# Layer 2's routing one group earlier, 16 scatters in every second group, and the tile list and padding beside the last scatters

## What is computed

```python
# layer 2, attention: 16 heads of 8 features, 64 queries and 64 keys for each batch entry, a mask
score = einsum('bhqd,bhkd->bhqk', qh, kh) / sqrt(8); attn = softmax(where(mask == 0, -1e9, score))
x = x + tanh(g_xattn[2]) * (merge(attn @ vh) @ w_o.T + b_o)
# layer 2, feed-forward: a LayerNorm of a LayerNorm, router, the 2 best of 8 experts, 128 -> 512 -> 128
xn = layer_norm(x_in) * gamma + beta          # x_in is itself the normed x; it is also the residual
probs = softmax(xn @ router_w.T / 1.5); w, idx = top_k(probs, 2)
out = sum over the 2 chosen e of w_e * (silu(xn @ W1[e]) @ W2[e]); x = x + tanh(g_ffn[2]) * (out + x_in)
```

## Time and profile before

| | us |
|---|---|
| median of 3 runs | 3185.36 |
| lowest, highest | 3180.08, 3189.39 |
| profiled execution, device time | 3190.76 |
| its span, first to last instruction | 3189.0 |
| layer 2 attention's group 3 to 14, at TensorE | 1682 to 1978 |
| last scatter issued | 2073.8 |
| first matmul of layer 2's feed-forward tiles | 2095.4 |

### The profile page before, as it was taken

One profiled execution on the slowest core, in us unless ns is written; L12 is line 12 of the kernel. 1 busy time (PEld: TensorE's weight loads), 2 busy tenths in 40 slices (PEclk: granted clock), 3 DMA queues, 4 the chain that ended last, 5 costly groups with the idle time before them and its releaser, 6 DMA issues. The chain is left out here.

```text
span 3189.0 us, 63316 instructions
## 1 busy us (share of the span) xinstructions
PE 2487.6 (78%) x20966; PEld 1889.2 (59%) x20966; DVE 2069.1 (65%) x6419; ACT 1395.7 (44%) x2573; POOL 1154.8 (36%) x1149
## 2 busy tenths in 40 slices
PE   3588778858779999999778888169996688887766
PEld 0254444447767787877656666147774365666755
DVE  6477648868667766677559788333333577784578
ACT  1466610013256666656456555022221465563432
POOL 2355512321054555455401344700000556634711
PEclk9988889969889999999989888579998788898988
DMA  4200001132100000000020010111111111100001
GB/s 142 98 31 27 20 27 40 39 113 70 34 1 1 1 1 1 0 1 1 16 71 12 28 36 23 46 47 54 53 54 53 43 33 32 39 10 10 1 25 33
DMA packets 126020, 108.78 MB, mean 34 GB/s; under 512 B 15548, under 2 KB 105942, under 8 KB 124888
## 3 DMA queue, kind: packets, MB, share of 16 engines
q1 hardware_dynamic: 106840, 80.58, 8.3%
q0 software_dynamic: 8192, 16.79, 1.8%
q10 hardware_dynamic: 10752, 8.39, 0.8%
HBM read 70.59 MB, written 35.13 MB: 33 GB/s over the span
## 5 line engine op out<-in xcount | busy, mean ns | idle before, releaser
L1318 POOL TENSOR_TENSOR l1ffn_hid<-l1ffn_act 128x512 f32<-128x512 f32 x256 | 330.5, 1294 | 341.7 <-ACT l1ffn_act L1459 308.0
L1600 DVE SCALAR_TENSOR_TENSOR l1ffn_acc<-bank,l1ffn_w,l1ffn_acc 128x128 f32<-128x128 f32 x960 | 269.3, 343 | 150.0 <-PE bank L1403 142.7
L1403 PEld LDWEIGHTS bank<-l_w_ahead,l1ffn_hid 128*128 128x128 f32 x2048 | 265.2, 191 | 68.7 <-issue 49.9
L1403 PE MATMUL bank<-l_w_ahead,l1ffn_hid 128*128 128x128 f32 x2048 | 271.7, 276 | 37.9 <-DVE l1ffn_acc L1600 37.5
L1456 ACT ACTIVATE l1ffn_act<-scores,l1ffn_b 128x512 f32<-128x512 f32 x256 | 176.3, 689 | 203.6 <-PE scores L214 203.4
L2231 ACT ACTIVATE l_probs_t<-bank 128x512 f32<-128x512 f32 x256 | 140.4, 596 | 105.9 <-PE bank L229 104.8
L2299 DVE TENSOR_REDUCE l_top<-scores 128x16 f32<-128x1024 f32 x128 | 155.2, 1213 | 43.1 <-PE scores L2130 42.6
L212 PE MATMUL scores<-l1ffn_z_high,l1ffn_w_high 128*128 128x512 f32 x384 | 173.5, 452 | 0.0
L2302 DVE TENSOR_TENSOR l_probs<-scores,l_top 128x1024 f32<-128x1024 f32 x128 | 156.8, 1225 | 13.7 <-DVE l_top L2299 0.5
L229 PEld LDWEIGHTS bank<-ident,l_probs 128*128 128x128 f32 x1024 | 130.0, 155 | 49.2 <-issue 25.5
L923 DVE SCALAR_TENSOR_TENSOR l0moe_acc<-scores,l0moe_w_now,l0moe_acc 128x128 f32<-128x128 f32 x512 | 137.7, 344 | 32.6 <-PE scores L871 32.6
(11 more groups left out here) (440 smaller groups left out, 6284.5 us busy)
## 6 DMA issues: line engine op xcount, KB each, us to landing
l2ffn_xs<-scratch_l_in SPq DMA_DIRECT2D x136, 64.0 KB, 1.8
scratch_l_out<-l2ffn_y SPq DMA_DIRECT2D x34, 256.0 KB, 2.3
x_all<-scratch_x SPq DMA_DIRECT2D x32, 256.0 KB, 3.4
l_ctx_t<-in_ctx_t SPq DMA_DIRECT2D x32, 256.0 KB
l_w_ahead<-in_l_w SPq DMA_DIRECT2D x3, 2048.0 KB, 12.7
x_all<-in_x SPq DMA_DIRECT2D x16, 256.0 KB, 3.0
l0mix_ctx<-in_ctx SPq DMA_DIRECT2D x16, 256.0 KB, 3.3
scratch_x<-l0mix_x_out ACTq DMA_DIRECT2D x16, 256.0 KB, 2.3
```

The source lines that it names most:

```text
L1318: pool.tensor_tensor(hid[:, e % K], act1[:, e % K], act3[:, e % K], ALU.mult)\
L1403: mm = pe.matmul(bank[5 + k][:, t * D:(t + 1) * D], hid[:, e % K, t * P:(t + 1) * P], w2[:, e, :], start=True, stop=True)
L1600: mm = v.scalar_tensor_tensor(out=acc[:, t, :], in0=y, scalar=w[:, h, t, e:e + 1], in1=before, op0=ALU.mult, op1=ALU.add)
```

## The change

It does four things.

1. The routing's steps move. The transposes of the routed z go from s = 3 to s = 1 of group i = g + 3; the logits from s = 1 of g + 4 to s = 2 of g + 3; `choose_first` from s = 2 of an odd group to s = 3 of the even group before it; `choose_second` from s = 3 of the odd group to s = 1 of it; the rank product from s = 2 of an even group to s = 3 of the odd group before it; `place_chosen` from s = 3 of an even group to its s = 0. Each `before` wait keeps its place in the slot; the waits on the routing's own readers move with the products.
2. A chunk's 16 scatters are issued in four successive slots, four in each, from s = 1 of an even group (6 for the first chunk) to s = 0 of the next; `LAG` is 6.
3. The count, the tile list and the padding writes are made at the end of the attention phase: TensorE's and VectorE's after their last slot, SyncE's after the context loads. The two tables for them are loaded with the routing's constants.
4. `l2_ffn` loses these steps; its SyncE waits for the padding and the scatters and loads at once.

```diff
 class PickTwo:
...
-    LAG = 7
+    LAG = 6
...
         sp.wait_ge(self.filled, 5)
         for e in range(picks.E):
             r = picks.E * picks.stride + e * P
-            sp.dma_start(picks.rows_in[r:r + P, :], self.zeros[:, :]).then_inc(self.padded, DMA)
-        sp.wait_ge(self.padded, picks.E * DMA)
+            sp.dma_start(picks.rows_in[r:r + P, :], self.zeros[:, :]).then_inc(picks.padded, DMA)
+
+    def pad(self, sp):
+        picks = self.picks
+        sp.wait_ge(self.listed, 1)
+        for e in range(picks.E):
+            r = sp.value_load(self.pad_row[0:1, e:e + 1], min_val=0, max_val=picks.E * picks.stride - P)
+            sp.dma_start(picks.rows_in[bass.ds(r, P), :], self.zeros[:, :]).then_inc(picks.padded, DMA)
+        sp.wait_ge(picks.padded, 2 * picks.E * DMA)
+
+    def tensor_count(self, pe):
+        pe.wait_ge(self.route, (self.CHUNKS - 1) * self.STEPS + 14)
+        pe.wait_ge(self.rank_out, self.CHUNKS)
+        pe.matmul(self.chip.bank[7][:, 0:L2_E], self.picks.ones[:, :], self.picks.cum[:, :, self.T], start=True, stop=True)\
+            .then_inc(self.counted, 1)
+
+    def vector_list(self, v):
+        picks, E, NT = self.picks, L2_E, self.picks.NT
+        full, past, before, tile_e, numbers = self.full, self.past, self.before, self.tile_e, self.numbers
+        n_tiles, ends = picks.n_tiles, picks.ends
+        total = self.chip.bank[7][:, 0:E]
+        made = 0
+
+        def next_step(instruction):
+            nonlocal made
+            made += 1
+            instruction.then_inc(self.table, 1)
+            v.wait_ge(self.table, made)
+        v.wait_ge(self.counted, 1)
+        v.tensor_tensor(self.pad_row[:, :], total, picks.base[:, :], ALU.add).then_inc(self.listed, 1)
+        next_step(v.tensor_tensor(full[:, :, :], self.steps[:, :].unsqueeze(1).to_broadcast([P, E, TILES]),
+                                  total.unsqueeze(2).to_broadcast([P, E, TILES]), ALU.is_lt))
+        next_step(v.tensor_reduce(n_tiles[:, :], full[:, :, :], AX.X, ALU.add))
+        next_step(v.tensor_tensor_scan(ends[:, :], picks.ones[:, 0:E], n_tiles[:, :], 0.0, ALU.mult, ALU.add))
+        next_step(v.tensor_tensor(past[:, :, :], numbers[:, :].unsqueeze(2).to_broadcast([P, NT, E]),
+                                  ends[:, :].unsqueeze(1).to_broadcast([P, NT, E]), ALU.is_ge))
+        next_step(v.tensor_reduce(tile_e[:, :], past[:, :, :], AX.X, ALU.add))
+        v.tensor_scalar(picks.tile_of_e[:, :], tile_e[:, :], float(E - 1), None, ALU.min).then_inc(self.listed, 1)
+        next_step(v.tensor_tensor(past[:, :, :], past[:, :, :],
+                                  n_tiles[:, :].unsqueeze(1).to_broadcast([P, NT, E]), ALU.mult))
+        next_step(v.tensor_reduce(before[:, :], past[:, :, :], AX.X, ALU.add))
+        next_step(v.tensor_tensor(before[:, :], numbers[:, :], before[:, :], ALU.subtract))
+        next_step(v.tensor_scalar(before[:, :], before[:, :], float(P), None, ALU.mult))
+        v.scalar_tensor_tensor(out=picks.tile_row[:, :], in0=tile_e[:, :], scalar=float(picks.stride),
+                               in1=before[:, :], op0=ALU.mult, op1=ALU.add).then_inc(self.listed, 1)
+        v.wait_ge(self.listed, 3)
 
...
-        c, part = divmod(i - 7, 2)
-        if 0 <= c < self.CHUNKS:
-            if part == 0 and s == 0:
+        c, part = divmod((i - 6) * G + s - 1, 2 * G)
+        if part < G and 0 <= c < self.CHUNKS:
+            if part == 0:
                 pool.wait_ge(self.routed, c + 1)
-            n = c * self.T + part * G + s
-            for k in range(picks.K):
-                pool.indirect_dma_start(out=picks.rows_in,
-                                        out_offset=bass.IndirectOffsetOnAxis(ap=picks.slot_in[:, k, n:n + 1], axis=0),
-                                        in_=picks.z[:, n, :], in_offset=None).then_inc(picks.scattered, DMA)
+            for n in (c * self.T + part * 2, c * self.T + part * 2 + 1):
+                for k in range(picks.K):
+                    pool.indirect_dma_start(
+                        out=picks.rows_in,
+                        out_offset=bass.IndirectOffsetOnAxis(ap=picks.slot_in[:, k, n:n + 1], axis=0),
+                        in_=picks.z[:, n, :], in_offset=None).then_inc(picks.scattered, DMA)
 
     def turned_out(self, pe, i):
         if 0 <= i - 3 < GROUPS:
             pe.wait_ge(self.z_t_done, i - 2)
 
     def logits_out(self, pe, i):
-        if 0 <= i - 4 < GROUPS:
-            pe.wait_ge(self.logits_done, i - 3)
+        if 0 <= i - 3 < GROUPS:
+            pe.wait_ge(self.logits_done, i - 2)
 
     def ranks_out(self, pe, i):
-        c, odd = divmod(i - 6, 2)
+        c, odd = divmod(i - 5, 2)
         if odd == 0 and 0 <= c < self.CHUNKS:
             pe.wait_ge(self.rank_out, c + 1)
 
     def tensor(self, pe, i, s, before):
 
         picks, bank, T, E = self.picks, self.chip.bank, self.T, L2_E
-        if s == 3 and 0 <= i - 3 < GROUPS:
+        if s == 1 and 0 <= i - 3 < GROUPS:
             g = i - 3
             pe.wait_ge(self.z_done, g * G + G)
             before()
             transposes(pe, bank[7], [picks.z[:, g * G + t, :] for t in range(G)], self.chip.ident)\
                 .then_inc(self.z_turned, 1)
-        if s == 1 and 0 <= i - 4 < GROUPS:
-            g = i - 4
+        if s == 2 and 0 <= i - 3 < GROUPS:
+            g = i - 3
             pe.wait_ge(self.z_t_done, g + 1)
             before()
             for t in range(G):
...
                     mm = pe.matmul(bank[7][r, t * E:(t + 1) * E], self.z_t[:, t * P + b * S:t * P + (b + 1) * S],
                                    picks.wr[:, :], start=True, stop=True)
             mm.then_inc(self.gated, 1)
-        c, odd = divmod(i - 6, 2)
-        if s == 2 and odd == 0 and 0 <= c < self.CHUNKS:
+        c, odd = divmod(i - 5, 2)
+        if s == 3 and odd == 0 and 0 <= c < self.CHUNKS:
             pe.wait_ge(self.route, c * self.STEPS + 14)
             before()
             out = bank[7][:, 0:T * E].rearrange("p (t e) -> p t e", t=T)
...
 
     def scalar(self, act, i, s):
         bank, T, E = self.chip.bank, self.T, L2_E
-        if s == 3 and 0 <= i - 3 < GROUPS:
+        if s == 1 and 0 <= i - 3 < GROUPS:
             g = i - 3
             act.wait_ge(self.z_turned, g + 1)
             reuse(act, self.gated, g)
             act.activation(self.z_t[:, :], bank[7][:, :], ACT.Identity, bias=self.picks.beta[:, 0:1],
                            scale=self.picks.gamma[:, 0:1]).then_inc(self.z_t_done, 1)
-        if s == 1 and 0 <= i - 4 < GROUPS:
-            g = i - 4
+        if s == 2 and 0 <= i - 3 < GROUPS:
+            g = i - 3
             act.wait_ge(self.gated, g + 1)
             reuse(act, self.route, (g // 2 - 2) * self.STEPS + 2)
             act.activation(self.logits[:, g // 2 % 2, g % 2 * G:(g % 2 + 1) * G, :].rearrange("p t e -> p (t e)"),
                            bank[7][:, 0:G * E], ACT.Identity).then_inc(self.logits_done, 1)
-        c, odd = divmod(i - 6, 2)
+        c, odd = divmod(i - 5, 2)
         if odd == 0 and 0 <= c < self.CHUNKS:
             if s == 0:
                 act.wait_ge(self.route, c * self.STEPS + 2)
                 act.activation(self.prob[:, :, :], self.shifted[:, :, :], ACT.Exp, scale=1.0 / L2_TEMP)\
                     .then_inc(self.exped, 1)
-            if s == 2:
+            if s == 3:
                 act.wait_ge(self.ranked, c + 1)
                 reuse(act, self.route, (c - 1) * self.STEPS + 17)
                 act.activation(self.rank[:, :, :].rearrange("p t e -> p (t e)"), bank[7][:, 0:T * E], ACT.Identity)\
                     .then_inc(self.rank_out, 1)
 
     def vector_setup(self, v):
-        v.wait_ge(self.w_in, 7 * DMA)
+        v.wait_ge(self.w_in, 9 * DMA)
         v.wait_ge(self.filled, 5)
 
     def vector(self, v, i, s):
...
             self.vector_stats(v, i - 2)
         if s == 0 and 0 <= i - 3 < GROUPS:
             self.vector_apply(v, i - 3)
+        c, odd = divmod(i - 4, 2)
+        if s == 3 and odd == 0 and 0 <= c < self.CHUNKS:
+            self.choose_first(v, c)
         c, odd = divmod(i - 5, 2)
-        if odd == 0 and 0 <= c < self.CHUNKS:
-            if s == 2:
-                self.choose_first(v, c)
-            if s == 3:
-                self.choose_second(v, c)
+        if s == 1 and odd == 0 and 0 <= c < self.CHUNKS:
+            self.choose_second(v, c)
         c, odd = divmod(i - 6, 2)
-        if s == 3 and odd == 0 and 0 <= c < self.CHUNKS:
+        if s == 0 and odd == 0 and 0 <= c < self.CHUNKS:
             self.place_chosen(v, c)
 
...
+                route.pad(sp)
...
                     if s == 0:
-                        route.turned_out(pe, i - 1)
+                        route.ranks_out(pe, i - 1)
                         group(i + 1, make_k)
                         tile(n, turn)
                         group(i - 1, lambda g: values(g * 2 + 1))
...
                         group(i - 1, turn_o)
```

(21 more changed lines are left out.)

## The result

| | before | after |
|---|---|---|
| median of 6 executions each | 3188.10 | 3222.15 |
| lowest, highest | 3180.08, 3194.08 | 3209.44, 3235.39 |
| profiled execution | 3190.76 | 3212.07 |
| TensorE, groups 3 to 14 from s = 1 | 295.34 | 332.22 |
| last scatter issued, to the first load's issue | 16.4 | 3.8 |

After over before is 1.0106, interval 1.0074 to 1.0138: slower by 34 us, where +13.5 was forecast, and above the range's upper end of 3218. The profiled execution of after shows 21.3 of the 34, and the seam above explains 21.7. It is the second fastest of its six (that of before is a seventh, beside its six). Where the slower ones lost the rest no trace shows, but their mean granted clock is on record, and it falls in the same order as the times rise: 0.892 at 3209.4 us, 0.891, 0.890, 0.887, 0.884, and 0.883 at 3235.4.

A forecast was written before the change was run, and what follows sets the result against it. It took TensorE and VectorE slots to bound the attention, and GpSimd's scatters, then list and padding, the seam's end. Attention +31.0, scatters -5.2, list -12.3 give +13.5: profiled 3190.8 to 3204.3, median 3198.9, range 3172 to 3218 us.

The forecast's parts named there:

- the clock term of the sum: Attention, groups 3 to 14: two of ten new TensorE waits bring a clock fall, net, adding 5.3 us.
- the carrying over of the profiled execution's surplus: Whole kernel: the profiled execution before lay 5.4 us above the median, so 3204.3 became a median forecast of 3198.9.
- The sizes in the attention: Groups 3 to 14: slot lengths sum to 321.0 against 295.3, +25.7, plus 5.3 for clock: +31.0 us.
- 9.05: Slot s = 2, groups 3 to 14: its length in us with the logits' wait before the values; lower end 8.0.
- The case held against falls: Group 11, s = 0 and s = 1: clock stayed 1.00 after group 10's stall, against all ten waits falling.
- The first rival: Attention: the clock falls in all ten new waits, +52.3 there, +34.8 in all, 3220.2 us; chance 0.17.
- The second rival: Attention: TensorE's clock stays up, only the order's own terms paid, +9.5; -8.0 in all, 3177.4 us; chance 0.20.
- The third: Attention, s = 2: the wait hides wholly behind VectorE's work; only the seam's 17.5 us counts, 3167.9; chance 0.13.
- The scatters: After the attention: 10 fewer scatters of 1.26 us each, two waits of 3.7 us for `place_chosen`: -5.2 us.
- The list and padding: End of seam: both fit beside the last scatters, so SyncE's first load follows the barrier: -12.3 us.
- the fourth rival: End of seam: the list doesn't leave the path, 12.3 us are not gained, 3211.2; chance 0.08.
- The bunching at no cost: Attention: 16 scatters take 20 us of GpSimd in each 50; issuing them bunched costs nothing.

## Why the prediction was wrong

**Two steps failed:** the clock term of the sum (17.9 us taken, some 24.3 paid), and the carrying over of the profiled execution's surplus of 5.4 us to the median (it was 2.7 for before and -10.1 for after). The cause of the second stays open.

**The place and the mechanism were right.** Twelve waits of 2.00 us before the logits, the values queued behind, VectorE idle for them: so forecast, and so the trace shows. The kernel before with that wait and nothing else lost 0.6%, and the kernel after without it lost nothing.

**The sizes in the attention were off by 5.9 us**, 36.9 against 31.0, and not where the sum had them. By kind of slot over groups 3 to 14, without the clock term (TensorE's slots, from the starts of the scores):

| slot | forecast | measured | |
|---|---|---|---|
| s = 2, 12 times | 108.6 | 106.6 | -2.0 |
| s = 1, 12 times | 64.2 | 72.2 | +8.0 |
| s = 3, 12 times | 70.4 | 71.2 | +0.8 |
| next s = 0, 12 times | 78.0 | 82.2 | +4.3 |
| clock, a term of its own | 5.3 | in the rows above | -5.3 |

- *The step of the sum that failed is the clock term:* "I take two of ten, net, 5.3". Of the ten named pauses eight were followed by a slot at 0.60 to 0.69: all five behind even s = 0, and three of five behind odd s = 1 (groups 9, 11 and 13). Three more falls came behind even s = 3 (0.74 to 0.75), a place that was not on the list. In the slot behind the pause they cost about 0.8, 2.9 and 1.3 us each at these three places, not 2.66 everywhere. With each slot at what the same kind of slot takes in this trace at a clock of 1.00, the twelve groups would last 307.9 us (an estimate from the trace's slots). So lower clock took some 24.3 us, where the forecast had 17.9 (5.3, and 12 x 1.05 in 9.05 over the full-clock 8.0). The rest of the sum is within 1 us of that estimate.
- *s = 2.* 9.05 was right only as a mean. At full clock the slot takes 7.95 (8.0 was the lower end); behind the pause of odd s = 1 it takes 10.8. That the two average out near 9.05 is luck.
- *s = 1.* VectorE's sum was right: "4.46 + 2.14 = 6.60" is what group 5 takes, at a clock of 1.00. Even s = 1 takes 5.44 in groups 8, 10, 12 and 14 because TensorE runs at 0.69. Odd s = 1 takes 7.07 in groups 9, 11 and 13 because the slot before it ran at 0.75, and VectorE waits for its values (1.43 us in group 9). Some 2 us are bookkeeping: 4.46 is VectorE's slot, TensorE's is 4.66, and the sum puts one beside TensorE's 9.05.
- *s = 0 of odd groups* takes 6.6 to 6.7 in groups 9, 11 and 13, forecast 5.40: the clock is 0.75 there after the wait at the end of s = 3.
- *The trace of before held the answer.* Its five pauses of 2.57 to 2.78 us at the start of s = 0 were followed by a fall in four, of which the prediction read one. The clock of s = 0 was 0.74, 0.60, 0.61, 1.00 and 0.74 in groups 6, 8, 10, 12 and 14; the stretches of groups 10 and 12 of before:

```profile
1843.24:1851.12 7.88, 7.88 (x95) 5.10 (x95) 5.21 (x12) 4.75 (x8) 2.13 (x3) 0.61 0.08 26
1894.84:1900.25 5.41, 5.13 (x94) 3.72 (x95) 5.27 (x13) 4.13 (x7) 2.13 (x3) 1.00 0.11 36
```

- The case held against falls, group 11's s = 0 and s = 1 at 1.00, began with a pause of 1.17 us and with none. And the falls make the twelve s = 0 of before 7.9 us longer than twelve times 5.40. They are in the 295.3 but not in the 321.0, so the +25.7 compares unlike sums.
- *The first rival* has the mechanism, at lower prices. Its 3220.2 is the nearest to the median, though the profiled execution reaches only 3212.1.
- *The second rival*, TensorE's clock staying up, falls: 0.87 over the stretch, and 3.65 us for values that take 2.06. The prediction leaned it on a sentence of the Trainium skill (TensorE: Matmul & The Clock Gate, Loop structure matters more than you think), which says "doesn't break PE warmth" of a loop whose next matmuls "follow immediately". That is not this case: TensorE stood idle for 2.8 to 3.1 us, and its clock fell. *The third*, the wait hidden by VectorE's other work, falls with the 64.2 us of VectorE's idle time.

**The scatters** gave 2.7 us (96.2 to 93.6 from group 15's s = 1 to the last of them) where -5.2 was forecast. The step itself held: from the end of the power of group 15's s = 3 it is 82.9 us before and 77.3 after, -5.6. Two waits for `place_chosen` came as foretold, 4.2 in place of 3.7 each. Single slow scatters cost 1.4 us above the usual (2.06 and 1.22 beside the list and padding), in before 2.3 (2.42 and 1.76); the idle time of 3.10 ahead of the last 15 is in both traces. What was lost is that the power starts 14.0 us after group 15's s = 1, where it was 11.1. In that group too the logits now stand ahead of the values, the values take 3.33 us in place of 2.05 at the lower clock, and VectorE waits for them. GpSimd of before, then VectorE of after, in order of time:

```profile
2055.19 0.97 POOL L1779 DMA_INDIRECT scratch_l_in<-l_r_z,l_r_slot_in  x1 [3.10 <-issue]
...
2030.86 0.36 DVE L2371 RECIPROCAL l_rsum<-bank 128x32 f32<-128x32 f32 x1 [2.92 <-PE bank L2220]
```

**The list and padding** gave 12.6 against 12.3, and 12.5 at the first matmul. This step was right in size and in mechanism, and the fourth rival is out: alone it was a gain of 0.3% on a second-kind chip.

**The bunching at no cost** was right on the first kind (335.8 with the scatters, 338.6 without) and wrong on the second, by 32 us (382 to 351 when spread). The rows of before, from one chip and with scatters mostly in runs of four, couldn't have shown it.

**The sum** at the seam was 13.5; it took 21.7 (21.3 over the whole profiled execution). Of the 8.2 between them 5.9 are the attention and 2.5 stand under the scatters (by the above, group 15's slower slots), less 0.3 for the list. The median is another 12.7 above that (34.1 less 21.3), and the median of before itself came out 2.7 higher with six executions than with three; together this is what lies between the forecast 3198.9 and 3222.2. The prediction carried the profiled execution's surplus of 5.4 over the median through unchanged; before's lies 2.7 above the median of the six, after's 10.1 below. So of the miss the larger part is that step, from one execution to the median. What the slower executions pay stays open; their lower mean clock, given with the result, is all that the record has on it.

## What to carry to other kernels

Before moving a product on an in-order engine, ask what its wait will stand in front of: a wait of 2.00 us for a shared PSUM bank, ahead of independent work, cost every group a VectorE idle time, and issuing that work first took the whole loss away and gained 0.6% even in the kernel before (on one chip of the second kind). Then list every pause of TensorE's in the trace you have, with the clock of the slot behind it, before you price a new one: here four of five pauses of 2.6 to 2.8 us were followed by a fall, and one was read. A helper's cheap part (list and padding beside the last scatters) is best taken alone: the part of this change that gained most was the one that moved nothing in the pipeline.

## What the runs showed of the hardware

- In the first chip's profile of after, all eleven pauses of TensorE of 2.8 to 3.1 us at the start of a slot, in groups 3 to 14, were followed by a slot at 0.60 to 0.75 of the clock. Shorter pauses were less certain: 2.57 us ahead of s = 2 of group 5 was followed by 1.00 there, and 2.57 to 2.61 at the same place by 0.78 to 0.80 in three other traces. In before 2.78 us was followed by 1.00 once (group 12). With the pause filled with work, s = 2 took 7.9 to 8.1 us in groups 7, 9, 11 and 13, where 10.8 was seen behind 3.05 us in 9 on the first chip. That it is the pause that brings the fall was not tried on the first kind.
- Two kinds of chip run the same program at 3190 and at 3307 to 3326 us, with the same times for the same unstalled slots. In layer 2's attention the difference comes with indirect scatters (for the order of after) and grows when they are issued in runs of eight: ScalarE idle for 7.9 us, the last 4.2 of them with its input ready. Nothing in the traces says what these engines wait for; the profile writes "remote". The rival named with the run without scatters, a stall that belongs to the place in the program, is out (339.8 us); whether the scatters hold up the loading of the engines' instructions isn't settled. It wasn't tried whether other DMA issues of GpSimd do the same.
- Most of the difference lies elsewhere: from the first feed-forward tile's result in layer 2 to ScalarE's first step of layer 3's MLP it is 774 to 785 us in the traces of the first kind and 864 to 876 in those of the second. That was not looked into.
